# Four attention and graph layers on one core: two layer norms on GpSimd, and one projection behind another

## What is computed

```
def _layernorm(x, axis=-1, eps=1e-05):
    m = jnp.mean(x, axis=axis, keepdims=True)
    v = jnp.var(x, axis=axis, keepdims=True)
    return (x - m) / jnp.sqrt(v + eps)

h = jnp.maximum(_layernorm(x, axis=-1), 0.0)
x = x + _L0_gnn_ref(h, adj, L0_gnn_W, L0_gnn_a)        # Wh = h W^T; s1 = Wh a1; s2 = Wh a2
h = jnp.maximum(_layernorm(x, axis=-1), 0.0)           # softmax of masked leaky_relu(s1 + s2), times Wh
x = x + _L1_gnn_ref(h, adj, L1_gnn_W, L1_gnn_b, L1_gnn_a)   # the same with four heads
h = jnp.maximum(_layernorm(x, axis=-1), 0.0)
x = x + _L2_gnn_ref(h, adj, ...)                       # sigmoid of pairwise scores, times h
h = jnp.maximum(_layernorm(x, axis=-1), 0.0)
x = x + _L3_gnn_ref(h, adj, ...)                       # three steps of a GRU over the edges
```

## Time and profile before

| | |
|---|---|
| median of 3 runs | 1065.44 us (1063.51 to 1066.78) |
| profiled execution, its own time | 1066.04 us |
| span of the profiled execution | 1063.9 us |
| granted TensorE clock, mean | 0.967 of full speed |
| PE busy | 954.6 us, 90% of the span |
| VectorE busy | 892.3 us, 84% |
| ScalarE busy | 864.0 us, 81% |
| GpSimd busy | 132.6 us, 12% |

### The profile page before, as it was taken

One profiled execution on the slowest core, in us unless ns is written; L12 is line 12 of the kernel. 1 busy time (PEld: TensorE's weight loads), 2 busy tenths in 40 slices (PEclk: granted clock), 3 DMA queues, 4 the chain that ended last, 5 costly groups with the idle time before them and its releaser, 6 DMA issues.

```text
span 1063.9 us, 16086 instructions
## 1 busy us (share of the span) xinstructions
PE 954.6 (90%) x5024; PEld 609.6 (57%) x5024; DVE 892.3 (84%) x2710; ACT 864.0 (81%) x1860; POOL 132.6 (12%) x170
## 2 busy tenths in 40 slices
PE   4588998999989899999989899998989999998866
PEld 3455565666566566656556566656656665655443
DVE  5296989899898979899897989989897989979543
ACT  3367888979888897988888897988889798887742
POOL 1102011010202011020201201020201101010000
PEclk8558999999999999999999999999999999999989
DMA  2401204021210403121220402121030302111000
GB/s 72 109 1 39 72 11 109 11 61 52 68 51 14 106 11 77 44 60 51 56 64 10 110 11 60 60 61 51 15 105 11 79 31 61 50 40 51 1 11 10
DMA packets 42477, 52.32 MB, mean 49 GB/s; under 512 B 1296, under 2 KB 25872, under 8 KB 42384
## 3 DMA queue, kind: packets, MB, share of 16 engines
q0 software_dynamic: 16896, 25.17, 10.7%
q1 hardware_dynamic: 17040, 21.83, 6.5%
q10 hardware_dynamic: 8448, 4.20, 1.3%
HBM read 55.39 MB, written 4.19 MB: 56 GB/s over the span
## 4 chain that ended last, share of the span: by engine, by line
PE 52%; DVE 28%; ACT 10%; issue 6%; POOL 3%; DMA 0%; DVEq 0%; SPq 0%; ACTq 0%; POOLq 0%
PE l_bank L948 7%; DVE probs L642 6%; PE a_bank L981 6%; PE x_bank L1040 4%; PE a_bank L948 3%; PE h_bank L1102 3%; ACT hn L394 3%; PE r_bank L1102 3%; PE r_bank L1105 3%; DVE sess L843 3%; DVE sess L836 3%; PE h_bank L1105 3%; PE n_bank L1105 3%; DVE probs L663 3%; POOL rstd L363 2%
## 5 line engine op out<-in xcount | busy, mean ns | idle before, releaser
L663 DVE SCALAR_TENSOR_TENSOR probs<-spread,s_lift,probs 128x512 f32<-128x512 f32 x320 | 237.4, 747 | 4.0 <-DVE rmax L642 0.5
L642 DVE CUSTOM_DVE_ANT_0 probs<-spread,mask 128x512 f32<-128x512 f32 x320 | 211.8, 684 | 2.4 <-ACT spread L450 2.3
L363 POOL TENSOR_TENSOR rstd<-var_eps,power 128x4 f32<-128x4 f32 x64 | 88.0, 1375 | 882.5 <-DVE var_eps L636 603.0
L460 ACT ACTIVATE probs<-probs,shift_p 128x512 f32<-128x512 f32 x256 | 185.7, 725 | 5.7 <-DVE shift_p L659 5.7
L468 ACT ACTIVATE pT<-l_bank 128x512 f32<-128x512 f32 x256 | 151.8, 600 | 46.5 <-PE l_bank L948 46.3
L948 PEld LDWEIGHTS l_bank<-ident,probs 128*128 128x128 f32 x1024 | 124.3, 144 | 73.8 <-issue 46.0
L948 PE MATMUL l_bank<-ident,probs 128*128 128x128 f32 x1024 | 150.5, 278 | 6.1 <-ACT probs L460 5.1
L394 ACT ACTIVATE hn<-x,shift,rstd 128x128 f32<-128x128 f32 x192 | 80.5, 492 | 26.1 <-POOL shift L365 26.0
L1005 PE MATMUL l_bank<-hT,dst_rep 128*128 128x512 f32 x128 | 73.6, 658 | 12.1 <-ACT pT L468 8.5
L870 DVE SCALAR_TENSOR_TENSOR hid_n<-r_t,hid_n 128x512 f32<-128x512 f32 x48 | 33.1, 689 | 57.8 <-ACT r_t L518 57.8
L981 PE MATMUL a_bank<-values,pT 128*128 128x128 f32 x512 | 65.7, 286 | 0.7 <-ACT pT L428 0.7
(11 more groups left out here) (175 smaller groups left out, 1956.5 us busy)
## 6 DMA issues: line engine op xcount, KB each, us to landing
adjt_i<-in_adj_t SPq DMA_DIRECT2D x16, 1024.0 KB, 5.2
edges<-in_adj POOLq DMA_DIRECT2D x16, 1024.0 KB, 5.9
adj_h<-in_adj POOLq DMA_DIRECT2D x16, 512.0 KB, 7.7
xin<-in_x SPq DMA_DIRECT2D x16, 256.0 KB, 2.9
out<-out_sb ACTq DMA_DIRECT2D x16, 256.0 KB, 3.8
weights_sb<-in_weights SPq DMA_DIRECT2D x1, 840.0 KB, 4.7
```

The lines of the kernel that those rows point to most:

```text
L363: g.tensor_tensor(rstd[n][:], var_eps[n][:], power[:], op=ALU.pow).then_inc(pool_step[n], 1)
L460: s.activation(row, row, ACT.Exp, bias=shift_p[:, head, c:c + 1], accum_out=den[:, head, c:c + 1]).then_inc(probs_ready, 1)
L642: return v.tensor_tensor_reduce(out=row, in0=spread_row, in1=mask, scale=1.0 / LIFT, scalar=-3e38, op0=ALU.subtract, op1=ALU.max, accum_ou ...
L663: v.scalar_tensor_tensor(row, spread_row, source, row, ALU.min, ALU.subtract, reverse1=True).then_inc(ready, 1)
```

## The change

The norms of layers 0 and 1 leave ScalarE. GpSimd subtracts the mean from all four chunks in one 128x512 instruction (new semaphore `centred`) and multiplies by `rstd` in another. `shift` and `minus_mean` of these two norms fall away. The ReLU moves into ScalarE's copy of the transposed tile to hT. The four steps `norm0_0` to `norm0_3` become one step `norm0`, and those of `norm1` one step `norm1`. Second, layer 0's `src0` goes behind `values0`: its step stands behind `m3` in the list, and the waits on `a_bank` follow: dst0, values0, src0, transposes.

```
-A_STEPS = (["stats0", "aggr0", "mean0"] + [f"norm0_{c}" for c in range(4)] + ["rows0", "mask0", "dst0", "src0", "values0"] + [f"m{c}" for c in range(4)]
-           + ["u0", "top0", "u1", "t0", "below0", "u2", "t1", "max0", "u3", "t2", "t3", "den0", "rden0"] + [f"sum0_{c}" for c in range(4)] + ["x1"])
+A_STEPS = (["stats0", "aggr0", "mean0"] + ["norm0"] + ["rows0", "mask0", "dst0", "values0"] + [f"m{c}" for c in range(4)]
+           + ["src0", "u0", "top0", "u1", "t0", "below0", "u2", "t1", "max0", "u3", "t2", "t3", "den0", "rden0"] + [f"sum0_{c}" for c in range(4)] + ["x1"])
...
@@ gpsimd
-                g.tensor_tensor(shift[n][:], minus_mean[n][:], rstd[n][:], op=ALU.mult).then_inc(ln_ready[n], 1)
+                if n >= 2:
+                    g.tensor_tensor(shift[n][:], minus_mean[n][:], rstd[n][:], op=ALU.mult).then_inc(ln_ready[n], 1)
+
+            def norm(p, n, rows):
+
+                if p.before().exists():
+                    pool.wait_ge(hT_ready[n], p.before().count(1, 1))
+                g.tensor_tensor(hn[n][:, :, :], rows, moments[n][:, :, 0:1].to_broadcast([P, C, D]),
+                                op=ALU.subtract).then_inc(centred[n], 1)
+                pool.wait_ge(centred[n], p.count(1, 1))
+                g.tensor_tensor(hn[n][:, :, :], hn[n][:, :, :], rstd[n][:, :].unsqueeze(2).to_broadcast([P, C, D]),
+                                op=ALU.mult).then_inc(hn_ready[n], 1)
...
+                if step == "norm0":
+                    norm(p, 0, xin[:, p.graph % 2, :, :])
+                if step == "norm1":
+                    norm(p, 1, x1[:, p.graph % 2, :, :])
@@ scalar
-                s.activation(hT[n][:, :], src[:, :], ACT.Copy).then_inc(hT_copied[n], 1)
+                s.activation(hT[n][:, :], src[:, :], ACT.Relu if n < 2 else ACT.Copy).then_inc(hT_copied[n], 1)
...
-                if step[:5] == "norm0":
-                    norm(p, 0, int(step[6]), xin[:, p.graph % 2, :, :])
-                elif step == "rows0":
+                if step == "rows0":
...
@@ vector
-                v.tensor_scalar(minus_mean[n][:, :], moments[n][:, :, 0], -1.0, None, ALU.mult)
+                if n >= 2:
+                    v.tensor_scalar(minus_mean[n][:, :], moments[n][:, :, 0], -1.0, None, ALU.mult)
...
@@ tensor
-                pe.wait_ge(hn_ready[n], p.count(C, C))
+                passes = C if n >= 2 else 1
+                pe.wait_ge(hn_ready[n], p.count(passes, passes))
...
                 elif step == "src0":
-                    pe.wait_ge(dst0_copied, p.count(1, 1))
+                    pe.wait_ge(val0_copied, p.count(1, 1))
...
                 elif step == "values0":
-                    pe.wait_ge(s10_copied, p.count(1, 1))
+                    pe.wait_ge(dst0_copied, p.count(1, 1))
...
                     if c == 0:
-                        pe.wait_ge(val0_copied, p.count(1, 1))
+                        pe.wait_ge(s10_copied, p.count(1, 1))
```

More of the change, by code:

```diff
@@ L20 @@
 PLAIN = 1024.0
-A_STEPS = (["stats0", "aggr0", "mean0"] + [f"norm0_{c}" for c in range(4)] + ["rows0", "mask0", "dst0", "src0", "values0"] + [f"m{c}" for c in range(4)]
-           + ["u0", "top0", "u1", "t0", "below0", "u2", "t1", "max0", "u3", "t2", "t3", "den0", "rden0"] + [f"sum0_{c}" for c in range(4)] + ["x1"])
-L_STEPS = (["stats1", "aggr1", "mean1"] + [f"norm1_{c}" for c in range(4)] + ["count", "rows1", "mask1", "dst1", "edges", "values1"]
+A_STEPS = (["stats0", "aggr0", "mean0"] + ["norm0"] + ["rows0", "mask0", "dst0", "values0"] + [f"m{c}" for c in range(4)]
+           + ["src0", "u0", "top0", "u1", "t0", "below0", "u2", "t1", "max0", "u3", "t2", "t3", "den0", "rden0"] + [f"sum0_{c}" for c in range(4)] + ["x1"])
+L_STEPS = (["stats1", "aggr1", "mean1"] + ["norm1"] + ["count", "rows1", "mask1", "dst1", "edges", "values1"]
            + [f"n{c}" for c in range(4)] + ["dst2"]
@@ L281, in graph_layers @@
         ln_ready = [sem(f"ln_ready{n}") for n in range(NORMS)]
+        centred = [sem(f"centred{n}") for n in range(2)]
         hn_ready = [sem(f"hn_ready{n}") for n in range(NORMS)]
@@ L432, in step_l @@
                 prev = p.before()
-                if step[:5] == "norm1":
-                    norm(p, 1, int(step[6]), x1[:, p.graph % 2, :, :])
-                elif step == "rows1":
+                if step == "rows1":
                     copy_hT(p, 1, l_bank0)
```

## The result

| | before | after |
|---|---|---|
| median of the runs of the comparison | 1065.42 us (1063.46 to 1067.75) | 1072.36 us (1070.37 to 1075.63) |
| profiled execution, its own time | 1066.04 us | 1075.63 us |
| granted TensorE clock in it | 0.967 | 0.953 |
| granted clock of the other seven runs of after | | 0.956 to 0.960 |

After takes 1.0068 times as long as before, with a 95% interval of 1.0056 to 1.008: 6.9 us between the medians. That is close to the forecast, and mostly by luck: the larger part of the loss has a reason that the prediction did not have. The profiled execution of after is the slowest of its eight, 3.3 us above their median, so its trace shows somewhat more of the loss than a usual run has.

The account below looks back on a forecast made before the run. No engine stood out; a chain of waits alternating between TensorE and VectorE was taken as the bound. Start -0.65, norm 1 of graph 0 +0.3 and lock +6.6 gave +6.3 us on 1065.44: 1071.7 us, range 1063 to 1081.

Parts of the forecast that it names:

- Part 1, norms off ScalarE: On ScalarE: 128 activations, 53 us of its 864, go; the gain was costed at nothing.
- Rival 2: Faster, as ScalarE was on the chain through norm 1's activations: 4.2 us less, 1061.2 us; chance 0.12.
- Part 2, the steady part: On TensorE from x3 to rows3, a fixed 6 us: removing the 1.36 us wait for s_lift gains zero.
- rival 4: The reordering gains nothing because an exponential takes the place of s_lift; counted within the forecast, with no chance of its own.
- Part 2, the start: Graph 0: maxima run in VectorE's idle time, logits begin at 20.0 instead of 20.68; gain 0.65 us, once.
- Part 3, the price of an instruction: On GpSimd: each 128x512 norm instruction with two SBUF operands was taken to cost 1.2 us.
- Rival 3: Slower by more: at 1.7 us a GpSimd instruction, L870 and L802 wait longer, +15.4 us, 1080.5; chance 0.15.
- Part 3, the lock: On VectorE's half of the chain: L802 waits for norm 0's SBUF access on GpSimd, +6.6 us in 13 graphs.
- rival 1: VectorE doesn't wait for GpSimd; only the start's -0.35 us is left, 1065.1 us; chance 0.33.
- Part 3, L870: On VectorE beside norm 1: held up by 0.65 us in about half the graphs, just covered, costing nothing.

Follow-up runs that it names:

- norm1_only: Only norm 1 moved to GpSimd, norm 0 and TensorE's order as in the kernel before; 1065.74 us, 1.0005 times before.
- src_fill_fit: The reordering of src0 alone, plus four dummy 128x512 TensorE products per graph between w3 and rows3; 1068.88 us, 1.0036 times before.
- src_only: Only src0 put behind values0, all norms left on ScalarE as in the kernel before; 1071.24 us, 1.0061 times before.
- norm0_only: Only norm 0 moved to GpSimd, norm 1 and TensorE's order as in the kernel before; 1068.04 us, 1.0021 times before.
- norm_only: Both norms moved to GpSimd, src0 still ahead of values0 as in the kernel before; 1069.05 us, 1.0045 times before.
- norm0_late: norm0_only plus a wait that keeps norm 0 behind L802, x2's add of the graph two ahead; 1069.41 us, 1.0038 times before.

## Why the prediction was right in its time and wrong in its reason

- **Part 1, norms off ScalarE: nothing.** It held. ScalarE lost 46 us, and hardly a graph got shorter: VectorE's half of graph 6 by 0.3 to 0.4 us in every kernel with a norm on GpSimd, and that of graph 12 by 0.3 in after. Rival 2, ScalarE on the chain, falls with norm1_only at 1.0005.
- **Part 2, the steady part: zero.** This is the step that failed. Its first half was read well: in undisturbed graphs the latency stays at 6.00 us, with an exponential in the place of `s_lift`, so rival 4 is right. But "whatever TensorE does within it, it waits at 488.44" looked only at when TensorE waits, and took its clock as given. With `values0` gone from between the units, the granted clock fell to half in one graph of three. Each of the four long dips costs about 1.6 us, the short one 0.3. These five are 6.7 of the 7.9 us by which after's middle grew, and src_fill_fit shows for the reordering alone that the time comes back without them. No term, rival or sign in the prediction named TensorE's clock.
- **Part 2, the start: -0.65.** Wrong. The logits of graph 0 were forecast for 20.0 and begin at 21.02 in after, 20.59 in src_only, against 20.68 in the earlier trace rows. The wait for `src0` at the end of the longer chain ate the gain:

```profile
20.82 0.16 DVE L692 TENSOR_SCALAR s_lift<-a_bank 128x4 f32<-128x4 f32 x1 [2.71 <-PE a_bank L952]
21.02 0.75 DVE L673 SCALAR_TENSOR_TENSOR probs<-spread,s_lift,probs 128x512 f32<-128x512 f32 x1
```

- **Part 3, the price of an instruction: 1.2 us.** It is 1.04 us alone and 1.05 to 1.08 in the mean, in the groups of GpSimd in after. The estimate from the Trainium skill's figure (GPSIMD Engine Reference, section 3.1), 1.12 us, was nearer than mine. Rival 3, which needed more than 1.25 us, is out.

```profile
L373 POOL TENSOR_TENSOR hn<-hn,rstd 128x512 f32<-128x512 f32 x32 | 34.7, 1083 | 2.5
L370 POOL TENSOR_TENSOR hn<-x,moments 128x512 f32<-128x512 f32 x16 | 17.1, 1071 | 1.2
L370 POOL TENSOR_TENSOR hn<-xin,moments 128x512 f32<-128x512 f32 x16 | 16.8, 1050 | 1.3
```

- **Part 3, the lock: +6.6 us on L802.** The mechanism was right, so rival 1 falls; the term was seven times too large. The records give 0.05 + 0.38 + 0.52 = 0.95 us. The 7 x 0.2 vanished because norm 0 is over after 2.1 us and not 2.5; of the six graphs reckoned at 1.4 to 1.8 us behind, two are there. On the chain the middle of norm0_only has 0.71.
- **Part 3, L870: covered.** Mostly so. It is held for 0.8 to 0.87 us in six graphs and for 0.1 in four, and norm1_only's middle grew by 0.32 us in all.

So 6.3 us were forecast as 6.6 for the lock less 0.35 at the start, and 6.9 came, chiefly from a clock that had no term. The lock term was 5.7 us too high, the missing term was 6.7 us in the trace, and that the two nearly cancel is luck.

**What stays open.** norm_only loses 5.2 us between the medians but 1.2 in the middle. Its trace has 0.2 more in the start and 1.5 in the rest, and the profiled execution of before was itself 2.2 us above the median that before has on norm_only's chip. Whether the norms make a low clock in the start and the rest likelier, or how the loss is shared among them otherwise, one trace for each kernel can't tell. Nor do the runs say why the dips come in one graph and not in the next, or how many a usual run of after has: its other runs had a clock of 0.956 to 0.960, against 0.953 in the trace.

## What to carry to other kernels

A wait of TensorE that is covered by a fixed latency isn't free to rearrange: look at what TensorE computes between its waits and how close together they lie, before and after, and not only at how long it waits. When a slower kernel has more TensorE busy time and no more TensorE work, look at the granted clock stretch by stretch first; then put back dummy work of the right size, with the same filler in the old kernel as the control, and count how many records the profile makes of one instruction before you size it. An engine that shares its access with a full one can't take over 128x512 work at its face value, and a wait that keeps it clear of one instruction sends it into the next.

## What the hardware showed unexpectedly

- The granted clock fell to half in mid-run, with TensorE busy for over 90% of the time. What it did just before the fall at 488.3 us was 1.30 us of waiting, four transposes and 0.53 of waiting. At 673 us, four more transposes and some records of one column lay between as well. With four products of 128 columns between the waits and the same 2.5 us of waiting in all, before has no dip from 108 to 1018 us.
- GpSimd holds VectorE as VectorE holds GpSimd: 128x512 with two SBUF operands took up to 1.56 us instead of 0.69. An instruction with one small operand can wait as well: in norm0_late, `minus_mean` (128x4) at 99.78 us took 0.96 us instead of 0.17, beside norm 0's second instruction from 99.68 to 100.72.
